# Transposes two steps behind their product, second products three, stores four, in a fused conditional-linear and ternary-FFN kernel

## The chip, the cores and the metric

One NeuronCore of a Trainium2 chip runs the whole program. The metric is the device time of one execution in microseconds, as the median of several runs. The engines are TensorE (PE in the profile; its weight loads are PEld), VectorE (DVE), ScalarE (ACT), GpSimd (POOL) and SyncE (SP), which here only issues DMAs.

## What is computed

128 elements of 128 rows and 512 columns. Each element has a category (0 to 63), which picks a 512x512 matrix and a bias. The result goes through a linear layer whose weights are rounded to -1, 0, 1 and whose activations are rounded to 8 bits by row; the output is added to x. Cut to what matters:

```python
cond = einsum('bsd,bdh->bsh', x, W[itok]) + b[itok][:, None, :]
w_scale = mean(abs(weight)) + 1e-8
w_quant = clip(round(weight / w_scale), -1, 1)
a_scale = max(abs(cond), axis=-1, keepdims=True) + 1e-8
a_quant = round(clip(cond / a_scale * 127, -128, 127))
y = einsum('bsi,oi->bso', a_quant, w_quant) * (w_scale * a_scale / 127)
out = x + y
```

## The kernel before

The kernel sorts the elements by category first, so that the weights of a category are loaded once, and writes the order into a table in SBUF (element numbers, "new category" flags, offsets into the rings of weights and biases). Then come 128 steps, one element each. `over_steps` writes them out as 8 first steps, a loop of 14 groups of 8, and 8 last steps; r is the step, u its place in the group.

A float32 product is done as three products of split operands (hi x hi, hi x lo, lo x hi). What each engine does in its step r, in the order in which it is written:

- **TensorE** (`body`, line 601): reads the offset of its weights from the table into a register (line 603, through `row_of`, line 165), waits for x_lo, for the seeded bias and for w_lo of step r, and issues the 12 matmuls of the **product** (lines 619 to 621) into one of four PSUM banks, `cond_ps`. Then `a_transpose(r-1)` (4 transposes, line 597, waits for the rounding of r-1 and for a free aT bank) and `second_product(r-2)` (4 matmuls, line 587, waits for `aT_moved` of r-2 and for the result of r-4, which frees one of two y banks).
- **VectorE** (`body`, line 523): absmax over the finished product r (line 527), step size and its inverse (lines 530, 533), `result(r-2)` (line 520: y times its scale plus x, in place in `x_rows`), then, only if step r+3 brings a new category, `split_low(r+3)`: two pieces of w_lo = w_raw - w_hi (line 486).
- **ScalarE** (`body`, line 399): `move(r-1)` (line 396, transposed values from PSUM to SBUF as bf16, waits for the transposes), the **rounding** of r (line 406, waits for the inverse), the **seed** of r+2 (line 346: the bias is copied into the bank of the product two steps ahead, `SEED_AHEAD` = 2), then, if step r+4 brings a new category, `split_high(r+4)`: two pieces of w_hi (line 355).
- **GpSimd** (`body`, line 323): splits x of step r+2 into x_hi and x_lo (lines 315, 317), and makes the output scale of r from absmax (line 334).
- **SyncE** (`body`, line 272), one queue: the store of r-3 (line 210, `STORE_BEHIND` = 3, waits for the result), then loads: transposed x of r+5 (waits for x_lo of r+1), rows of x of r+1 into a ring of 8 slots (line 284 waits until the store of the slot's last user, step r-7, has landed), and weights and bias of r+6 if they are new (waits for w_lo of r+2).

The rings: 4 slots of weights, 8 of biases, 4 of x, of rounded activations and of aT, 4 of the row scales, 8 of `x_rows`, 4 product banks, 2 banks each for y and aT. All engines run their own queue in order; they are tied by semaphores only. After step 127 the last transposes, second products, results and stores are written out (lines 627 to 630, 408, 545, 290).

Of the kernel before, what the change touches and what calls it, by code (L numbers as in the profile page):

```python
# [26 lines left out]
def adaln_ffn(nc, x, x_t, itok, cond_w, cond_b, ffn_t, out):  # L27
    B, S, D = x.shape
# [6 lines left out]
    U = 8  # L35
    W_RING, BIAS_RING, XT_RING, Q_RING, STAT_RING = 4, 8, 4, 4, 4
    COND_BANKS, PS_RING = 4, 2
    LO_AHEAD, HI_AHEAD, W_AHEAD, XT_AHEAD, ROWS_AHEAD = 3, 4, 6, 5, 1
    X_AHEAD, SEED_AHEAD, Y_BEHIND, STORE_BEHIND = 2, 2, 2, 3
    PIECES = 2  # L40
    PIECE = W_FREE // PIECES
    BUSY = 12
# [2 lines left out]
    with ctx:  # L45
# [293 lines left out]
        @block.scalar  # L339
        def _(act):  # L340
            def bias_slot(step):
                (bias_offset,) = row_of(act, step, BIAS_OFFSET, 1)
                return bounded(act, bias_offset, (BIAS_RING - 1) * H)

            def seed(bias_offset, n):
                act.activation(cond_ps[n % COND_BANKS][:, :], bias[:, bass.ds(bias_offset, H)],  # L346
                               ACT.Copy).then_inc(bias_seeded, 1)

            def split_high(new, offset, step, n):

                with act.If(new > 0):
                    act.wait_ge(w_loaded[n], w_landed(step, n))
                    for piece in range(PIECES):
                        at = offset + piece * PIECE
                        act.activation(w_hi[:, bass.ds(at, PIECE)], w_raw[:, bass.ds(at, PIECE)],  # L355
                                       ACT.Copy).then_inc(w_hi_done, 1)
                with act.Else():

                    if type(step) is not int or step > 1:
                        act.wait_ge(w_hi_done, (step - 1) * PIECES)  # L360
                    act.sem_inc(w_hi_done, PIECES)

            act.wait_ge(consts_done, 3)
            act.activation(marks[:, 0:1], rounder[:, :], ACT.Abs)
            act.wait_ge(elements_mm_done, 1)
            for column, behind in ((XT_ELEMENT, W_AHEAD - XT_AHEAD), (ROWS_ELEMENT, W_AHEAD - ROWS_AHEAD),
                                   (OUT_ELEMENT, W_AHEAD + STORE_BEHIND)):
                act.activation(table[:, behind:behind + B, column], y_ps[1][0:1, 0:B],
                               ACT.Copy).then_inc(elements_done, 1)
            act.wait_ge(ffn_loaded, 16)  # L370
            act.activation(ffn_abs[:, :], ffn_raw[:, :], ACT.Abs,
                           accum_out=ffn_sum[:, 0:1]).then_inc(ffn_summed, 1)
            for k in range(KD):
                act.wait_ge(w0_loaded[k], 16)
                act.activation(w_hi[:, k * H:(k + 1) * H], w_raw[:, k * H:(k + 1) * H],
                               ACT.Copy).then_inc(w0_hi_done, 1)
                if k == 0:
                    act.wait_ge(banks_opened, COND_BANKS)
                    act.wait_ge(bias0_loaded, 16)
                    seed(0, 0)  # L380
            act.wait_ge(table_done, 1)
            for step in range(1, HI_AHEAD):
                new, offset = w_slot(act, step)
                if step < SEED_AHEAD:
                    bias_offset = bias_slot(step)
                split_high(new, offset, step, step)
                if step < SEED_AHEAD:
                    act.wait_ge(w_loaded[step], 32)
                    seed(bias_offset, step)

            def move(step, n, first):

                act.wait_ge(aT_done, step + 1)
                if not first or n >= Q_RING:
                    act.wait_ge(y_mm_done, step - Q_RING + 1)
                act.activation(aT[:, n % Q_RING, :], aT_ps[n % PS_RING][:, 0:H].bitcast(I16), ACT.Copy,  # L396
                               bias=-HALF_OFFSET).then_inc(aT_moved, 1)

            def body(r0, u, first, last):
                r = r0 + u  # L400
                if not first or u:
                    move(r - 1, (u - 1) % U, first)
                if not first or u >= Q_RING:
                    act.wait_ge(aT_done, r - Q_RING + 1)
                act.wait_ge(a_inv_done, r + 1)
                act.activation(a_rounded[:, u % Q_RING, :], cond_ps[u % COND_BANKS][:, :], ACT.Identity,  # L406
                               bias=rounder[:, 0:1], scale=a_inv[:, u % STAT_RING:u % STAT_RING + 1]).then_inc(a_rounded_done, 1)
                if last and u == U - 1:
                    move(r, u, False)
                if not last or u + SEED_AHEAD < U:  # L410
                    bias_offset = bias_slot(r + SEED_AHEAD)
                    n = (u + SEED_AHEAD) % U
                    act.wait_ge(w_loaded[n], w_landed(r + SEED_AHEAD, n))
                    seed(bias_offset, n)
                if not last or u + HI_AHEAD < U:
                    new, offset = w_slot(act, r + HI_AHEAD)
                    split_high(new, offset, r + HI_AHEAD, (u + HI_AHEAD) % U)

            over_steps(act, body)

        @block.vector
        def _(dve):
# [100 lines left out]
            def body(r0, u, first, last):  # L523
                r = r0 + u
                s = u % STAT_RING
                dve.wait_ge(cond_mm_done, r + 1)
                dve.tensor_reduce(absmax[:, s:s + 1], cond_ps[u % COND_BANKS][:, :], AX.X, ALU.max,  # L527
                                  apply_absolute_value=True).then_inc(absmax_done, 1)
                dve.wait_ge(absmax_done, r + 1)
                dve.tensor_scalar(a_step[:, s:s + 1], absmax[:, s:s + 1], EPS, 1.0 / LEVELS,  # L530
                                  ALU.add, ALU.mult).then_inc(a_step_done, 1)
                dve.wait_ge(a_step_done, r + 1)
                dve.reciprocal(a_inv[:, s:s + 1], a_step[:, s:s + 1]).then_inc(a_inv_done, 1)  # L533
                if first and u == 0:
                    ternary_begin()
                elif first and u == 1:
                    ternary_end()
                else:
                    result(r - Y_BEHIND, (u - Y_BEHIND) % U)
                if not last or u + LO_AHEAD < U:  # L540
                    new, offset = w_slot(dve, r + LO_AHEAD)
                    split_low(new, offset, r + LO_AHEAD)
# [6 lines left out]
        def _(pe):  # L549
# [51 lines left out]
            def body(r0, u, first, last):  # L601
                r = r0 + u
                _, offset = w_slot(pe, r)
                start = first and u == 0
                pe.wait_ge(x_lo_done, r + 1)
                pe.wait_ge(bias_seeded, r + 1)
                n = u % XT_RING
                for k in range(KD):
                    if start:
                        pe.wait_ge(w0_lo_done, k + 1)  # L610
                    elif k * PIECES % KD == 0:

                        pe.wait_ge(w_lo_done, (r - 1) * PIECES + k * PIECES // KD + 1)
                    x_hi_k = xT_hi[:, n, k * P:(k + 1) * P]
                    x_lo_k = xT_lo[:, n, k * P:(k + 1) * P]
                    w_hi_k = w_hi[:, bass.ds(offset + k * H, H)]
                    w_lo_k = w_lo[:, bass.ds(offset + k * H, H)]
                    ps_cond = cond_ps[u % COND_BANKS][:, :]
                    pe.matmul(ps_cond, x_hi_k, w_hi_k, start=False, stop=False, skip_group_check=True)  # L619
                    pe.matmul(ps_cond, x_hi_k, w_lo_k, start=False, stop=False, skip_group_check=True)  # L620
                    last_mm = pe.matmul(ps_cond, x_lo_k, w_hi_k, start=False, stop=(k == KD - 1), skip_group_check=True)  # L621
                last_mm.then_inc(cond_mm_done, 1)
                if not first or u >= 1:
                    a_transpose(r - 1, (u - 1) % U, first)
                if not first or u >= Y_BEHIND:
                    second_product(r - Y_BEHIND, (u - Y_BEHIND) % U, first)
                if last and u == U - 1:
                    second_product(r - 1, u - 1, False)
                    a_transpose(r, u, False)
                    second_product(r, u, False)  # L630

            over_steps(pe, body)


# [24 lines left out]
```

## Time and profile before

| | |
|---|---|
| median of 3 runs (lowest, highest) | 546.17 us (544.36, 547.55) |
| profiled execution | 543.38 us, span 541.5 us |
| TensorE busy | 512.7 us (95%) |
| VectorE busy | 392.5 us (72%) |
| ScalarE busy | 343.7 us (63%) |
| GpSimd busy | 281.2 us (52%) |
| moved by DMA | 172.76 MB, mean 319 GB/s |
| mean granted TensorE clock | 0.998 of full speed |

The span is the time from the first to the last instruction on the core. Matmuls overlap in the pipeline, and their ends are modelled, so 95% busy does not mean that TensorE issues without gaps: the starts of successive matmuls tell more. A wait in the list of waits is the idle time of an engine just ahead of an instruction, with the last releaser that the trace knows; "issue" means that it knows none. Names with q (PEldq, DVEq) are an engine's sequencer, which reads registers and waits, and is not counted as busy.

### The profile page before, as it was taken

The page shows a single profiled execution, that of the slowest core. Times are in us where ns is not written, and L with a number is a line of the kernel's source. Part 1 is how long each engine was busy: PE and PEld are TensorE (multiplying, and loading weights), DVE is VectorE, ACT ScalarE, POOL GpSimd, SP SyncE. Part 2 cuts the span into 40 slices and gives each one's busy share as a digit, 9 for nine tenths or more (in the row PEclk, how much of TensorE's full clock was granted, in tenths as well). Part 3 has the DMA queues.
Part 4 walks back from the last instruction along what each step waited for, and adds up shares of the span by engine and source line. Part 5 has one row for each costly group of instructions (what it writes and reads, how often), then busy time and mean ns, then how long its engine had stood idle before and what let it go on. Part 6 is the DMA issues. An engine that isn't in the chain of part 4 may idle for free.

```text
span 541.5 us, 13855 instructions
## 1 busy us (share of the span) xinstructions
PE 512.7 (95%) x2584; PEld 355.8 (66%) x2585; DVE 392.5 (72%) x652; ACT 343.7 (63%) x502; POOL 281.2 (52%) x396
## 2 busy tenths in 40 slices
PE   4799999999999999999999998999989999999996
PEld 1576667666776666677676665667657677777774
DVE  3787765879667968966866858776797868758763
ACT  3577565765676567666756666766766666666753
POOL 3695455444556364555554463555446455565540
PEclk9999999999999999999999999999999999999999
DMA  5899879998899999979989889987999999899963
GB/s 170 276 404 351 291 258 310 382 364 274 324 364 343 367 333 392 356 243 372 350 291 294 325 322 398 365 288 271 407 332 363 329 363 342 273 310 333 323 194 117
DMA packets 71728, 172.76 MB, mean 319 GB/s; under 512 B 8096, under 2 KB 8224, under 8 KB 64800
## 3 DMA queue, kind: packets, MB, share of 16 engines
q1 hardware_dynamic: 71712, 172.59, 90.0%
q8 instruction: 5, 0.08, 0.1%
q14 instruction: 11, 0.09, 0.1%
HBM read 139.00 MB, written 33.55 MB: 319 GB/s over the span
## 4 chain that ended last, share of the span: by engine, by line
PE 35%; DVE 6%; issue 5%; DVEq 2%; ACT 2%; DMA 2%; ACTq 0%; SPq 0%; POOL 0%; POOLq 0%
PE ps_cond L619 9%; PE ps_cond L621 8%; PE ps_cond L620 8%; PE ps_y L587 8%; DVE sb_w_lo L486 3%; PE ps_aT L597 2%; DVE sb_absmax L527 2%; DMA sb_bias<-cond_b 2%; DVEq L165 1%; ACT sb_a_rounded L406 1%; ACT sb_w_hi L355 1%; DVE sb_a_step L530 0%; ACTq L165 0%; DVE sb_x_rows L520 0%; DVEq L486 0%
## 5 line engine op out<-in xcount | busy, mean ns | idle before, releaser
L619 PE MATMUL ps_cond<-sb_w_hi,sb_xT_hi 128*128 x512 | 220.7, 431 | 6.7 <-issue 3.2
L621 PE MATMUL ps_cond<-sb_w_hi,sb_xT_lo 128*128 x512 | 200.3, 391 | 0.0
L620 PE MATMUL ps_cond<-sb_w_lo,sb_xT_hi 128*128 x512 | 199.4, 389 | 0.0
L486 DVE TENSOR_TENSOR sb_w_lo<-sb_w_raw,sb_w_hi x106 | 162.1, 1567 | 20.2 <-issue 16.8
L317 POOL TENSOR_TENSOR sb_xT_lo<-sb_xT_raw,sb_xT_hi 128x512 fp32r<-128x512 f32 x128 | 166.4, 1300 | 10.9
L527 DVE TENSOR_REDUCE sb_absmax<-ps_cond 128x1 f32<-128x512 f32 x128 | 87.7, 686 | 100.6 <-PE ps_cond L621 89.1
L406 ACT ACTIVATE sb_a_rounded<-ps_cond,sb_rounder,sb_a_inv 128x512 f32<-128x512 f32 x128 | 99.5, 777 | 94.9 <-DVE sb_a_inv L533 94.5
L334 POOL TENSOR_SCALAR sb_y_scale<-sb_absmax,sb_w_step 128x1 f32<-128x1 f32 x128 | 41.0, 320 | 224.6 <-DVE sb_absmax L527 224.3
L587 PE MATMUL ps_y<-sb_ffnT,sb_aT 128*128 128x512 bf16 x512 | 131.2, 379 | 1.6 <-DVE sb_ffnT L512 0.9
L619 PEld LDWEIGHTS ps_cond<-sb_w_hi,sb_xT_hi 128*128 128x128 f32 x512 | 96.2, 188 | 51.7 <-issue 27.2
L396 ACT ACTIVATE sb_aT<-ps_aT 128x512 bf16<-128x512 int16 x128 | 75.4, 589 | 67.5 <-PE ps_aT L597 62.8
L355 ACT ACTIVATE sb_w_hi<-sb_w_raw x106 | 106.3, 1051 | 14.9 <-issue 9.2
L621 PEld LDWEIGHTS ps_cond<-sb_w_hi,sb_xT_lo 128*128 128x128 f32 x512 | 96.0, 188 | 21.7
L620 PEld LDWEIGHTS ps_cond<-sb_w_lo,sb_xT_hi 128*128 128x128 f32 x512 | 96.4, 188 | 18.0
L520 DVE SCALAR_TENSOR_TENSOR sb_x_rows<-ps_y,sb_y_scale,sb_x_rows 128x512 f32<-128x512 f32 x128 | 96.1, 751 | 6.4 <-PE ps_y L587 1.7
L315 POOL CAST sb_xT_hi<-sb_xT_raw 128x512 fp32r<-128x512 f32 x128 | 78.2, 611 | 17.8 <-DMA sb_xT_raw<-x_t 12.5
L346 ACT ACTIVATE ps_cond<-sb_bias 128x512 f32 (+1 forms) x128 | 76.2, 595 | 7.6 <-issue 6.2
L587 PEld LDWEIGHTS ps_y<-sb_ffnT,sb_aT 128*128 128x128 bf16 x512 | 44.6, 98 | 32.4 <-ACT sb_aT L396 1.2
L597 PE MATMUL ps_aT<-sb_ident_bf,sb_a_rounded 128*128 128x128 bf16 x512 | 50.9, 222 | 9.9 <-ACT sb_a_rounded L406 9.7
L597 PEld LDWEIGHTS ps_aT<-sb_ident_bf,sb_a_rounded 128*128 128x128 bf16 x512 | 29.0, 98 | 46.3 <-issue 24.8
L533 DVE RECIPROCAL sb_a_inv<-sb_a_step 128x1 f32<-128x1 f32 x128 | 20.9, 164 | 4.4
L530 DVE TENSOR_SCALAR sb_a_step<-sb_absmax 128x1 f32<-128x1 f32 x128 | 19.7, 154 | 4.4
(69 smaller groups left out, 36.2 us busy)
## 6 DMA issues: line engine op xcount, KB each, us to landing
sb_w_raw<-cond_w SPq DMA_DIRECT2D x53, 1024.0 KB, 6.6
sb_xT_raw<-x_t SPq DMA_DIRECT2D x128, 256.0 KB, 5.1
sb_x_rows<-x SPq DMA_DIRECT2D x128, 256.0 KB, 5.2
out<-sb_x_rows SPq DMA_DIRECT2D x128, 256.0 KB, 4.9
sb_bias<-cond_b SPq DMA_DIRECT2D x54, 256.0 KB, 7.9
sb_ffn_raw<-ffn_t SPq DMA_DIRECT2D x1, 1024.0 KB, 6.9
sb_w_raw<-cond_w SPq DMA_DIRECT2D x4, 256.0 KB, 6.7
sb_cat_row_i<-itok SPq DMA_DIRECT2D x1, 64.0 KB, 3.5
```

The source lines that it names most:

```text
L315: pool.tensor_copy(xT_hi[:, m, :], xT_raw[:, m, :]).then_inc(x_hi_done, 1)
L317: pool.tensor_tensor(xT_lo[:, m, :], xT_raw[:, m, :], xT_hi[:, m, :].bitcast(F32), ALU.subtract).then_inc(x_lo_done, 1)
L355: act.activation(w_hi[:, bass.ds(at, PIECE)], w_raw[:, bass.ds(at, PIECE)], ACT.Copy).then_inc(w_hi_done, 1)
L406: act.activation(a_rounded[:, u % Q_RING, :], cond_ps[u % COND_BANKS][:, :], ACT.Identity, bias=rounder[:, 0:1], scale=a_inv[:, u % STAT_R ...
L486: dve.tensor_tensor(w_lo[:, bass.ds(at, PIECE)], w_raw[:, bass.ds(at, PIECE)], w_hi[:, bass.ds(at, PIECE)].bitcast(F32), ALU.subtract).the ...
L520: dve.scalar_tensor_tensor(x_rows[:, n, :], y_ps[n % PS_RING][:, :], y_scale[:, s:s + 1], x_rows[:, n, :], ALU.mult, ALU.add).then_inc(y_d ...
L527: dve.tensor_reduce(absmax[:, s:s + 1], cond_ps[u % COND_BANKS][:, :], AX.X, ALU.max, apply_absolute_value=True).then_inc(absmax_done, 1)
L587: last_mm = pe.matmul(y_ps[n % PS_RING][:, :], aT[:, n % Q_RING, k * P:(k + 1) * P], ffnT[:, k, :], start=(k == 0), stop=(k == KH - 1))
L597: last_t = pe.transpose(aT_ps[n % PS_RING][:, k * P:(k + 1) * P], low[:, k * P:(k + 1) * P, 0], ident_bf[:, :])
L619: pe.matmul(ps_cond, x_hi_k, w_hi_k, start=False, stop=False, skip_group_check=True)
L620: pe.matmul(ps_cond, x_hi_k, w_lo_k, start=False, stop=False, skip_group_check=True)
L621: last_mm = pe.matmul(ps_cond, x_lo_k, w_hi_k, start=False, stop=(k == KD - 1), skip_group_check=True)
```

## The change

`T_BEHIND` = 2 is new: in step r TensorE transposes the rounded activation of r-2 instead of r-1, and ScalarE moves that of r-2. `Y_BEHIND` goes from 2 to 3: TensorE does the second product, and VectorE the result, of r-3 instead of r-2. `STORE_BEHIND` goes from 3 to 4, which also makes the table one row longer. The first steps leave out what isn't there yet, and after the last step one more transposition, second product, move and result are written out. Ring sizes and how far ahead anything is loaded, split or seeded stay.

```diff
--- before.py
+++ after.py
@@ -36,7 +36,7 @@
     W_RING, BIAS_RING, XT_RING, Q_RING, STAT_RING = 4, 8, 4, 4, 4
     COND_BANKS, PS_RING = 4, 2
     LO_AHEAD, HI_AHEAD, W_AHEAD, XT_AHEAD, ROWS_AHEAD = 3, 4, 6, 5, 1
-    X_AHEAD, SEED_AHEAD, Y_BEHIND, STORE_BEHIND = 2, 2, 2, 3
+    X_AHEAD, SEED_AHEAD, T_BEHIND, Y_BEHIND, STORE_BEHIND = 2, 2, 2, 3, 4
     PIECES = 2
     PIECE = W_FREE // PIECES
     BUSY = 12
@@ -398,15 +398,16 @@
 
             def body(r0, u, first, last):
                 r = r0 + u
-                if not first or u:
-                    move(r - 1, (u - 1) % U, first)
+                if not first or u >= T_BEHIND:
+                    move(r - T_BEHIND, (u - T_BEHIND) % U, first)
                 if not first or u >= Q_RING:
                     act.wait_ge(aT_done, r - Q_RING + 1)
                 act.wait_ge(a_inv_done, r + 1)
                 act.activation(a_rounded[:, u % Q_RING, :], cond_ps[u % COND_BANKS][:, :], ACT.Identity,
                                bias=rounder[:, 0:1], scale=a_inv[:, u % STAT_RING:u % STAT_RING + 1]).then_inc(a_rounded_done, 1)
                 if last and u == U - 1:
-                    move(r, u, False)
+                    for n in range(U - T_BEHIND, U):
+                        move(B - U + n, n, False)
                 if not last or u + SEED_AHEAD < U:
                     bias_offset = bias_slot(r + SEED_AHEAD)
                     n = (u + SEED_AHEAD) % U
@@ -535,7 +536,7 @@
                     ternary_begin()
                 elif first and u == 1:
                     ternary_end()
-                else:
+                elif not first or u >= Y_BEHIND:
                     result(r - Y_BEHIND, (u - Y_BEHIND) % U)
                 if not last or u + LO_AHEAD < U:
                     new, offset = w_slot(dve, r + LO_AHEAD)
@@ -620,11 +621,13 @@
                     pe.matmul(ps_cond, x_hi_k, w_lo_k, start=False, stop=False, skip_group_check=True)
                     last_mm = pe.matmul(ps_cond, x_lo_k, w_hi_k, start=False, stop=(k == KD - 1), skip_group_check=True)
                 last_mm.then_inc(cond_mm_done, 1)
-                if not first or u >= 1:
-                    a_transpose(r - 1, (u - 1) % U, first)
+                if not first or u >= T_BEHIND:
+                    a_transpose(r - T_BEHIND, (u - T_BEHIND) % U, first)
                 if not first or u >= Y_BEHIND:
                     second_product(r - Y_BEHIND, (u - Y_BEHIND) % U, first)
                 if last and u == U - 1:
+                    a_transpose(r - 1, u - 1, False)
+                    second_product(r - 2, u - 2, False)
                     second_product(r - 1, u - 1, False)
                     a_transpose(r, u, False)
                     second_product(r, u, False)
```

## Rows read from the trace of the kernel before

**Rows 1.** The page: span, busy time of each engine (share) xinstructions, DMA totals.
```profile
span 541.5 us, 13855 instructions
...
PE 512.7 (95%) x2584; PEld 355.8 (66%) x2585; DVE 392.5 (72%) x652; ACT 343.7 (63%) x502; POOL 281.2 (52%) x396
...
DMA packets 71728, 172.76 MB, mean 319 GB/s; under 512 B 8096, under 2 KB 8224, under 8 KB 64800
```

**Rows 2.** The page, chain that ended last: shares of the span by engine.
```profile
PE 35%; DVE 6%; issue 5%; DVEq 2%; ACT 2%; DMA 2%; ACTq 0%; SPq 0%; POOL 0%; POOLq 0%
```

**Rows 3.** Waits, whole span: engine and line waited for, total us, times, longest.
```profile
PEld ps_cond L619 <- issue: 27.2, 52, 1.5
...
PE ps_aT L597 <- ACT sb_a_rounded L406: 9.7, 14, 1.0
```

**Rows 4.** Timeline of PE: first matmuls of products 6, 126 and 127 (start us, us).
```profile
39.32 0.58 PE L619 MATMUL ps_cond<-sb_w_hi,sb_xT_hi 128*128 x1
...
527.00 0.58 PE L619 MATMUL ps_cond<-sb_w_hi,sb_xT_hi 128*128 x1
...
530.85 0.58 PE L619 MATMUL ps_cond<-sb_w_hi,sb_xT_hi 128*128 x1
```

**Rows 5.** Timeline of PE: product 27, transposes, second product, product 28.
```profile
124.67 0.53 PE L619 MATMUL ps_cond<-sb_w_hi,sb_xT_hi 128*128 x1
...
128.65 0.40 PE L597 MATMUL ps_aT<-sb_ident_bf,sb_a_rounded 128*128 128x128 bf16 x4 [0.94 <-ACT sb_a_rounded L406]
128.89 1.03 PE L587 MATMUL ps_y<-sb_ffnT,sb_aT 128*128 128x512 bf16 x4
129.90 0.49 PE L619 MATMUL ps_cond<-sb_w_hi,sb_xT_hi 128*128 x1
```

**Rows 6.** Timeline of VectorE over three of its steps.
```profile
121.45 0.68 DVE L527 TENSOR_REDUCE sb_absmax<-ps_cond 128x1 f32<-128x512 f32 x1
...
123.44 3.29 DVE L486 TENSOR_TENSOR sb_w_lo<-sb_w_raw,sb_w_hi  x2 [0.23 <-issue]
126.66 0.68 DVE L527 TENSOR_REDUCE sb_absmax<-ps_cond 128x1 f32<-128x512 f32 x1
...
128.85 0.69 DVE L527 TENSOR_REDUCE sb_absmax<-ps_cond 128x1 f32<-128x512 f32 x1 [0.36 <-DVEq L492]
```

**Rows 7.** The page, groups of instructions: VectorE splits of weights.
```profile
L486 DVE TENSOR_TENSOR sb_w_lo<-sb_w_raw,sb_w_hi x106 | 162.1, 1567 | 20.2 <-issue 16.8
```

**Rows 8.** Timeline of ScalarE: rounding and bias seed.
```profile
127.82 0.78 ACT L406 ACTIVATE sb_a_rounded<-ps_cond,sb_rounder,sb_a_inv 128x512 f32<-128x512 f32 x1 [3.01 <-DVE sb_a_inv L533]
128.50 0.59 ACT L346 ACTIVATE ps_cond<-sb_bias 128x512 f32 x1
```

**Rows 9.** Source line 165, PE's sequencer (ns min/median/max): whole span, then 49.9 to 50.1.
```profile
L165 PEldq TENSOR_LOAD <-sb_table x128: 532/538/2149, 11.5 to 528.4; - x128
...
L165 PEldq TENSOR_LOAD <-sb_table x1: 1467/1467/1467, 50.0 to 50.0; - x1
```

**Rows 10.** Timeline of PE in the first steps, before product 3.
```profile
25.73 0.40 PE L597 MATMUL ps_aT<-sb_ident_bf,sb_a_rounded 128*128 128x128 bf16 x4
27.05 1.02 PE L587 MATMUL ps_y<-sb_ffnT,sb_aT 128*128 128x512 bf16 x4 [0.92 <-DVE sb_ffnT L512]
27.86 0.50 PE L619 MATMUL ps_cond<-sb_w_hi,sb_xT_hi 128*128 x1
```

**Rows 11.** Windows: first steps (last columns: PEclk, DMA share, GB/s).
```profile
22.90:39.30 16.40, 15.48 (x83) 10.97 (x81) 14.34 (x21) 11.50 (x17) 15.97 (x14) 1.00 1.00 373
```

**Rows 12.** Timeline of the end: ScalarE, PE, VectorE.
```profile
535.16 0.78 ACT L406 ACTIVATE sb_a_rounded<-ps_cond,sb_rounder,sb_a_inv 128x512 f32<-128x512 f32 x1 [0.34 <-DVE sb_a_inv L533]
...
537.08 1.04 PE L587 MATMUL ps_y<-sb_ffnT,sb_aT 128*128 128x512 bf16 x4 [0.69 <-ACT sb_aT L396]
...
538.15 0.75 DVE L520 SCALAR_TENSOR_TENSOR sb_x_rows<-ps_y,sb_y_scale,sb_x_rows 128x512 f32<-128x512 f32 x1 [1.45 <-PE ps_y L587]
```

**Rows 13.** Source line 210, stores: us from issue to landing.
```profile
DMA to landing us min/median/max: 2.0/4.9/8.1
```

## The prediction

> **What bounds the kernel now.** The page comes first: TensorE is busy for 95% of 541.5 us, VectorE for 72%, and 172.76 MB move at a mean of 319 GB/s [rows 1]. A mean like that hides stages, so the chain of waits comes next. PE holds 35% of it, and the rest of what can be named is mostly VectorE and "issue" [rows 2]. In the list of waits the reader is to see two kinds of PE stall: transposes that wait for the rounding (9.7 us, 14 times, none over 1.0), and the first weight load of a product, which waits for nothing that the profile shows (27.2 us, 52 times) [rows 3]. Second, the pace. An undisturbed step is 3.85 us, from product to product [rows 4]. Product 6 starts at 39.32 and product 127 at 530.85 [rows 4]: 491.5 us for 121 steps, which undisturbed would be 465.3. So the middle of the kernel holds **26.3 us of stall**. That is what can be won there.
>
> Where does it come from? A VectorE step that also splits weights lasts 5.21 us (absmax at 121.45, the next one at 126.66); one that does not can be followed by the next absmax after 2.19 (126.66 to 128.85) [rows 6]. 106 pieces of w_lo are 53 splitting steps [rows 7]. In the timeline they fall into 22 single ones, 11 pairs and 3 triples. One split puts VectorE 5.21 - 3.85 = 1.36 us behind PE, and the next plain step makes it good. Two in a row put it 2.7 behind, and then PE stops. Product 27 starts at 124.67, and its 12 matmuls are over in time for transposes 2.9 us later, but these start at 128.65, released by the rounding. Then come second product and the next product, at 129.90: 5.23 us for the step, **1.38 lost** [rows 5]. 11 pairs at 1.38, and 3 triples at 1.38 + 1.36 = 2.74, are 23.4 of the 26.3 us. 2.9 are left for single splits and for register loads.
>
> **The change, part by part.**
>
> *Transposes two steps behind.* No instruction is added. Each step still has its 12 matmuls, 4 transposes and 4 matmuls of the second product, so the floor of 3.85 stays, and PE cannot gain from it. What goes is the wait: after product r the transposes want the rounding of r-2, a whole step old, not that of r-1. What is late next? The bias that ScalarE copies into the bank of product r+1. It stands behind the same rounding in ScalarE's queue, since it is seeded two steps ahead, as before. In the stalled step the rounding starts at 127.82, the seed at 128.50, and the seed ends at 129.09 [rows 8]. Without the change the following product starts at 129.90 [rows 5]. With it, the transposes and the second product run while the seed is awaited, and the product starts as soon as the seed is there. How long after it the trace doesn't show. The lower bound is the 0.05 from the end of a rounding (127.82 + 0.78) to the transposes at 128.65; the upper bound is a whole register load of 0.54 [rows 9]. I take 0.35, nearer the upper end because PE's sequencer still has the product's other waits and address computations to do. So 129.44 for 129.90: **0.46 us** (0.27 to 0.76).
>
> This is won once for each backlog, not once a step. While VectorE is behind without a break, its own 5.21 a step sets the pace, and a PE that can run further ahead only moves the start of the stall. So 11 + 3 = 14 times 0.46 = **6.4 us** (3.8 to 10.6).
>
> *The sequencer's lead.* Ahead of each product PE's sequencer reads the table of offsets: 538 ns in the median, but up to 2149, and one of 1467 stands for several others [rows 9]. Its long cases are hidden only if it is reached early, and the sequencer reaches it after the waits of the transposes. Today these end with the rounding of r-1, so after any single split (VectorE 1.36 late) the read comes late and its excess shows as "issue" [rows 3]. Afterwards the wait ahead of it is for a move of aT which ScalarE does ahead of that rounding. With the 0.05 to 0.15 that a single split costs, this is what the remaining 2.9 us are made of. I take **2.0** (0 to 2.9).
> The Trainium skill (TensorE: Matmul & The Clock Gate, Architectural detail) gives TensorE a queue of 64 instructions, which is more than the 40 loads and matmuls of a step. By that rule the sequencer could be a step ahead, all long reads would vanish, and this term would be 2.9. No row here shows the depth of the queue.
>
> *Second products three steps behind, in VectorE too.* VectorE's result(r-3) stands where result(r-2) stood, and its second product is again the one that PE issues in the same step, so this wait keeps its place. The second product waits for the move of r-3, which ScalarE does at the head of step r-1, as it did that of r-2 before. The bank of y is freed by the result of r-5 in VectorE's step r-2, as before. The four-slot rings of aT, a_rounded and of the scales are enough, and no bank of cond is held longer. Cost 0. All of it lies beside PE's products.
>
> *Start.* Step 1 has no transposes, step 2 no second product. Today the second product of row 0 stands there until ternary ffnT is done (27.05, idle 0.92), and product 3 starts at 27.86, although the transposes ahead were issued at 25.73 [rows 10]. Afterwards product 3 can start at 25.73 + 0.23 = 25.96. It keeps up to 1.9, for VectorE loses its result in step 2 as well (0.75) and so isn't the next bound. But the DMA engines are busy for a share of 1.00 in this stretch [rows 11], and the loads may hold it: I take **1.5** (0 to 1.9).
>
> *End.* One more transposition and second product are left over. The move of 126 now stands behind the rounding of 127 in ScalarE's queue (535.16 + 0.78). So it runs from about 535.8 to 536.4, second product 126 from 536.5 to 537.3, transposes 127 after that, their move to 538.4, and the last second product starts at about 538.45 instead of 537.08 [rows 12]. **1.4 us lost** (1.1 to 1.6), and the last result at 538.15 moves with it.
>
> *Stores four behind.* SP waits for y_done of r-4, which VectorE sets in step r-1, as it did for r-3: the wait is not later. The loads of x_t, x and weights behind it in SP's queue keep their places. What gets shorter is the time from a store to the reuse of its x_rows slot: three steps, 11.5 us, instead of four. The slowest store landed after 8.1 us [rows 13]. Cost 0; if that cover were gone, SP would stand there with the weight load behind it.
>
> **Sum**: 6.4 + 2.0 + 1.5 - 1.4 = **8.5 us**. The profiled execution was 543.4 us (span 541.5 and 1.9 around it) and would be 534.9. The median of the runs is 546.17, 2.8 above it. I set the gain against it: **537.7**. By the ends of the terms: 3.8 + 0 + 0 - 1.6 = 2.2 to 10.6 + 2.9 + 1.9 - 1.1 = 14.3, that is 531.9 to 544.0.
>
> **The rivals.**
> *The seed takes the whole place of the rounding.* If a product that was held by its seed starts as late as it does now (0.8 us after the seed's end), the 14 backlogs give nothing. For: both hang on one rounding, 0.68 us apart. Against: 1.25 us of PE work lies between transposes and product, and now overlaps the wait. Start and end cancel: about 546.
>
> *The transfers are the bound where weights come thick.* For: the share of 1.00 at the start [rows 11], a mean of 319 GB/s [rows 1]. Pairs and triples are just where a megabyte of weights a step is loaded. Against: among the longest waits of VectorE and ScalarE none of size is for a DMA. Half of the backlogs' gain and the start would go: 537.7 + 3.2 + 1.5 = 542.4.
> The Trainium skill (Perfetto Trace Analysis, Roofline) puts the ceiling of one core's 16 DMA engines at about 435 GB/s. By it 172.76 MB need some 397 us, and this rival has room only in short stretches.
>
> *Slower: the stores.* With a slot needed again after 11.5 us, a store that lands later stops SP, and with it the weight loads behind. It decides from a landing of 11.2 us on, 3.1 above the slowest. Prefetch of six steps absorbs the first of it. If each of the 14 dense stretches then loses 1 us: 546.2 - 8.5 + 14 = 551.7.
>
> *More than forecast*: seeds hardly hold PE and all long reads are hidden: 532 to 533.
>
> **How the numbers follow.** Forecast 0.72, seeds 0.10, transfers 0.09, stores 0.05, more 0.04. A difference of under 0.5% (2.7 us) can't be told from none here. Faster by more than that, under 543.4: nearly all of the forecast, about all of "more" and half of "transfers", 0.81. Within it 0.14, slower 0.05. The range of 8 in 10 is 533.5 to 544.0.
>
> **What would show it right or wrong.** Transposes have no wait for the rounding left in the list of waits. Steps that come after pairs of splits take 4.7 to 4.8 us instead of 5.2, and the wait moves to L619. PE's 121 steps from product 6 to 127 take 483 us instead of 491.5. The last second product starts some 7.6 us after the last product, instead of 6.2 (537.08 less 530.85). It is wrong if steps after pairs stay at 5.2, if ScalarE's w_hi starts to wait for DMA, or if SP waits for stores within the loop.

## The result, and the profile after

The changed kernel takes **538.49 us** (median of 4 runs, 537.63 to 540.65) against 545.81 for the kernel before (4 runs, 544.36 to 547.55). The ratio is 0.987, with a 95% interval from 0.984 to 0.990: 7.3 us faster, forecast 8.5. The predicted 537.7 is 0.8 us off. The profiled execution went from 543.38 to 539.01, its span from 541.5 to 537.2. That is 4.4 us and not 7.3, because the profiled execution of before was quicker than all four of its timed runs (544.36 and up). So what is read below from one pair of traces is checked, where it matters, against the other traces of kernels with the same lag.

First the page and the waits of the changed kernel, which answer to [rows 1] and [rows 3]. Line numbers behind the change are one higher than before: 598 are the transposes, 588 the second product, 620 to 622 the product.

```profile
span 537.2 us, 13884 instructions
...
PE 508.2 (95%) x2584; PEld 356.9 (66%) x2585; DVE 386.9 (72%) x652; ACT 343.2 (64%) x502; POOL 280.2 (52%) x396
```

```profile
PEld ps_cond L620 <- issue: 31.4, 33, 2.0
...
PE ps_cond L620 <- ACT ps_cond L346: 10.7, 14, 1.6
ACT sb_w_hi L355 <- DMA sb_bias<-cond_b: 7.8, 8, 1.4
...
PEld ps_aT L598 <- ACT sb_a_rounded L406: 7.1, 27, 0.3
```

The transposes' wait for the rounding has left PE's own list. What remains of it on PEld is never over 0.3 us. In its place a new row stands: 14 times the product waits for its seed, 10.7 us in all. (The row with "issue" doesn't mean that no cause is known: its longest cases are weight loads of products whose first matmul shows the seed.) ScalarE's waits of w_hi for a transfer are 7.8 us, 8 times; before they were 4.0 us, 5 times. The prediction had named this as a sign of being wrong; it is there, but small.

The stalled step of [rows 5] and [rows 8] in the changed kernel, first PE, then ScalarE:

```profile
122.79 0.58 PE L620 MATMUL ps_cond<-sb_w_hi,sb_xT_hi 128*128 x1
...
125.72 0.40 PE L598 MATMUL ps_aT<-sb_ident_bf,sb_a_rounded 128*128 128x128 bf16 x4
125.96 1.03 PE L588 MATMUL ps_y<-sb_ffnT,sb_aT 128*128 128x512 bf16 x4
127.60 0.49 PE L620 MATMUL ps_cond<-sb_w_hi,sb_xT_hi 128*128 x1 [0.62 <-ACT ps_cond L346]
```

```profile
125.99 0.78 ACT L406 ACTIVATE sb_a_rounded<-ps_cond,sb_rounder,sb_a_inv 128x512 f32<-128x512 f32 x1 [2.13 <-DVE sb_a_inv L534]
126.67 0.59 ACT L346 ACTIVATE ps_cond<-sb_bias 128x512 f32 x1
```

The transposes run 2.93 us after the product's start, although the rounding for which they waited before, that of product 26, only begins at 125.99. The seed ends at 127.26, and the product follows 0.34 us later. The step lasts 4.81 us instead of 5.23.

Products 6 and 127, which answer to [rows 4]:

```profile
39.31 0.58 PE L620 MATMUL ps_cond<-sb_w_hi,sb_xT_hi 128*128 x1
...
525.13 0.58 PE L620 MATMUL ps_cond<-sb_w_hi,sb_xT_hi 128*128 x1
```

The 121 steps between take 485.8 us instead of 491.5, that is **20.6 us over the floor** instead of 26.3. Forecast was 483. (The floor of 465.3 is 121 steps of 3.845 us; the median step of either trace is 3.847.) Single traces differ by about 1 us here, so three of each kind are worth a look. With transposes one step behind, the loss over the floor is 26.3 us in the kernel before and 27.6 in each of two variants below that time the same (a part of the change, and the seed first). With two behind it is 20.6 in the changed kernel and 19.5 and 20.4 in two variants that time the same (the early read, and second products four behind). The means are 27.2 and 20.2: **7.0 us**, which fits the medians better than 5.7.

### The profile page after: what moved, and what is told of

Read it like the earlier page. It is cut to its first block and busy times, and to the rows that moved or that the text cites. A ratio compares the mean times of both kernels' runs of the same rounds, so it can differ in the third digit from the quotient of the medians.

```text
span 537.2 us, 13884 instructions
## 1 busy us (share of the span) xinstructions
PE 508.2 (95%) x2584; PEld 356.9 (66%) x2585; DVE 386.9 (72%) x652; ACT 343.2 (64%) x502; POOL 280.2 (52%) x396
## 5 line engine op out<-in xcount | busy, mean ns | idle before, releaser
L620 PE MATMUL ps_cond<-sb_w_hi,sb_xT_hi 128*128 x512 | 221.9, 433 | 16.7 <-ACT ps_cond L346 10.7
L487 DVE TENSOR_TENSOR sb_w_lo<-sb_w_raw,sb_w_hi x106 | 156.2, 1512 | 28.8 <-issue 22.0
L355 ACT ACTIVATE sb_w_hi<-sb_w_raw x106 | 106.4, 1052 | 20.6 <-issue 11.2
```

The lines of the kernel that those rows point to most:

```text
L487: dve.tensor_tensor(w_lo[:, bass.ds(at, PIECE)], w_raw[:, bass.ds(at, PIECE)], w_hi[:, bass.ds(at, PIECE)].bitcast(F32), ALU.subtract).the ...
```

## The experiments

Each was timed in turn with the kernel before on the same chip, and its ratio is to the kernel before of that session, whose median was 547.21, 545.88, 546.01 and 545.26 us in the four sessions. Differences to the changed kernel are between sessions: they are good to 1 or 2 us.

**Only a part: transposes stay one step behind.**

```diff
-    X_AHEAD, SEED_AHEAD, T_BEHIND, Y_BEHIND, STORE_BEHIND = 2, 2, 2, 3, 4
+    X_AHEAD, SEED_AHEAD, T_BEHIND, Y_BEHIND, STORE_BEHIND = 2, 2, 1, 3, 4
...
-                    a_transpose(r - 1, u - 1, False)
```

> Only a part of the change: second products three steps behind and stores four, but transposes one step behind, as before. Theory (the gain comes from the transposes' wait alone): 545 to 548, no gain in the middle, the transposes still wait for the rounding some 14 times. Rival (the second product's wait for the move, or the result's place on VectorE, was part of what held PE): at least half of the 7 us gained.

547.64 us, ratio 1.002 (0.999 to 1.005). As expected, nothing is gained, and the wait is what it was before:

```profile
PEld ps_aT L598 <- ACT sb_a_rounded L406: 25.5, 41, 2.2
...
PE ps_aT L598 <- ACT sb_a_rounded L406: 12.5, 14, 1.8
```

**Only a part: stores four behind on the kernel before.**

```diff
-    X_AHEAD, SEED_AHEAD, Y_BEHIND, STORE_BEHIND = 2, 2, 2, 3
+    X_AHEAD, SEED_AHEAD, Y_BEHIND, STORE_BEHIND = 2, 2, 2, 4
```

> The kernel before with the stores alone four steps behind; second products two, transposes one. SP then waits for a result made a step earlier. With stores three behind on the changed kernel ScalarE waited 91 us for weights, so SP's place against VectorE matters. Theory (loads are held by w_lo, their ring's release, in the same VectorE step, as soon as the store does not hold them): within 1.5 us of before. Rival (SP's waits of 26.1 us for results delay the weights already in the kernel before, and part of the change's gain is the store's alone): 3 us or more faster than before.

547.86 us, ratio 1.005 (1.003 to 1.007): no gain, but a loss of 2 us, a little more than the theory's 1.5. Its cause was not looked for. The stores alone are no part of the gain.

**The change without its part on the stores.**

```diff
-    X_AHEAD, SEED_AHEAD, T_BEHIND, Y_BEHIND, STORE_BEHIND = 2, 2, 2, 3, 4
+    X_AHEAD, SEED_AHEAD, T_BEHIND, Y_BEHIND, STORE_BEHIND = 2, 2, 2, 3, 3
```

> The changed kernel with stores three steps behind instead of four: SP then waits for a result that VectorE makes in the same step and not in the one before, with the loads behind it in SP's queue. Theory (loads have steps of slack): within 1.5 us of the changed kernel, 537 to 541. Rival (SP's queue is late enough that weights arrive late; four behind is a needed part of the change): 3 us or more slower than the changed kernel.

563.67 us, ratio 1.029 (1.024 to 1.035). The theory fell by far: this is some 25 us slower than the changed kernel. Waits of SP, then of ScalarE:

```profile
SPq L210 <- DVE sb_x_rows L521: 66.2, 47, 3.5
```

```profile
ACT sb_w_hi L355 <- DMA sb_bias<-cond_b: 91.1, 51, 5.1
```

SP now waits for a result of the same VectorE step (66.2 us; in the changed kernel 21.7), and the weight load stands behind this wait in its queue. ScalarE then waits 91.1 us for weights instead of 7.8. The six steps of prefetch are no slack here: a load can only be issued when the split of w_lo has freed its slot, and with one more VectorE step of delay behind that the weights come too late.

**One step more for the stores.** The same line with `STORE_BEHIND` = 5.

> The changed kernel with stores five steps behind. SP no longer waits for a result (21.7 us, 19 times in the changed kernel), but a slot of x_rows is needed again two steps, 7.7 us, after its store was issued, and the slowest of before landed after 8.1. Theory (loads are held by the release of the weight ring, and nearly all stores land in time): within 2 us of the changed kernel. Rival one (the store's slot decides): 4 us or more slower, with waits of SP for stores. Rival two (SP's waits for results cost time): 3 us or more faster.

541.24 us, ratio 0.989 (0.985 to 0.994), so the changed kernel's time within the noise, or up to 3 us more. SP's wait for results fell to 13.0 us, and its wait for the split rose from 14.6 to 25.1, so the loads leave no earlier. SP never waited for a store's slot inside the loop:

```profile
SPq L230 <- DVE sb_w_lo L487: 25.1, 15, 2.9
SPq L210 <- DVE sb_x_rows L521: 13.0, 9, 3.0
```

**The seed ahead of the rounding, in the changed kernel.**

```diff
             def body(r0, u, first, last):
                 r = r0 + u
+                if not last or u + SEED_AHEAD < U:
+                    bias_offset = bias_slot(r + SEED_AHEAD)
+                    n = (u + SEED_AHEAD) % U
+                    if not first or u + SEED_AHEAD >= COND_BANKS:
+                        act.wait_ge(a_rounded_done, r + SEED_AHEAD - COND_BANKS + 1)
+                    act.wait_ge(w_loaded[n], w_landed(r + SEED_AHEAD, n))
+                    seed(bias_offset, n)
                 if not first or u >= T_BEHIND:
                     move(r - T_BEHIND, (u - T_BEHIND) % U, first)
...
-                if not last or u + SEED_AHEAD < U:
-                    bias_offset = bias_slot(r + SEED_AHEAD)
-                    n = (u + SEED_AHEAD) % U
-                    act.wait_ge(w_loaded[n], w_landed(r + SEED_AHEAD, n))
-                    seed(bias_offset, n)
```

> The changed kernel, but ScalarE seeds the bank of step r+2 at the head of its step r, ahead of the move and of the rounding of r. Theory (the seed behind the rounding holds PE where VectorE is late: 14 waits of the product for the seed, 10.7 us, and 0.34 us from the seed's end to the product in each): the product's wait for the seed goes, steps after a pair of splits fall from 4.8 us to near 3.85, and the whole falls by 8 to 15 us against the changed kernel, to 524 to 531. Rival (VectorE's 5.21 us per splitting step is the bound wherever splits are dense, so no queue order can help): within 2 us of the changed kernel.

532.23 us, ratio 0.973 (0.968 to 0.977): 6.3 us under the changed kernel by the medians, 7.9 by the ratios. The direction is the theory's, the size just short of it. Between products 6 and 127 the loss over the floor is 14.1 us. PE's wait for the seed is down from 10.7 to 1.3 us, and two others have come forward:

```profile
ACT sb_w_hi L355 <- DMA sb_bias<-cond_b: 26.2, 27, 2.0
...
PEld ps_y L590 <- ACT sb_aT L396: 8.3, 11, 1.6
...
PE ps_y L590 <- ACT sb_aT L396: 6.0, 10, 1.4
...
PE ps_cond L622 <- ACT ps_cond L346: 1.3, 2, 0.8
```

**The same in the kernel before.**

> The kernel before, with the same move of the seed to the head of ScalarE's step. Theory (transposes one step behind wait for the rounding of VectorE's late step, whatever the seed does): no gain, 544 to 548, and steps after a pair stay at 5.2 us. Rival (it was the seed all along that held PE, and the lag of the transposes is only a small part): some 8 us or more faster than before.

547.02 us, ratio 0.998 (0.996 to 1.001). No gain, as expected. The transposes' lag and the seed's place hold the same backlog one behind the other. Taking away the second alone gives nothing, and taking away the first alone only uncovers the second.

**A further step for the second products, with the seed first.**

```diff
-    W_RING, BIAS_RING, XT_RING, Q_RING, STAT_RING = 4, 8, 4, 4, 4
+    W_RING, BIAS_RING, XT_RING, Q_RING, STAT_RING = 4, 8, 4, 4, 8
...
-    LO_AHEAD, HI_AHEAD, W_AHEAD, XT_AHEAD, ROWS_AHEAD = 3, 4, 6, 5, 1
-    X_AHEAD, SEED_AHEAD, T_BEHIND, Y_BEHIND, STORE_BEHIND = 2, 2, 2, 3, 4
+    LO_AHEAD, HI_AHEAD, W_AHEAD, XT_AHEAD, ROWS_AHEAD = 3, 4, 6, 5, 0
+    X_AHEAD, SEED_AHEAD, T_BEHIND, Y_BEHIND, STORE_BEHIND = 2, 2, 2, 4, 5
...
-            load_rows(element, 0)
...
+                    second_product(r - 3, u - 3, False)
```

> The changed kernel with the seed first, second products and results four steps behind, stores five; rows of x are loaded in their own step instead of one ahead, which keeps three steps between a store and the reuse of its slot, and the row scales have 8 slots. With the seed first, the second product waits 14.3 us for the move of aT (8.3 of its weight loads, 6.0 of its matmuls), which stands behind w_hi. Theory (that move is the next bound): 3 to 7 us faster than with the seed first alone (532.2), 525 to 529. Rival (ScalarE is held by weights from DMA, 26.2 us, and the stall moves to the next instruction): within 1.5 us of 532.

526.55 us, ratio 0.963 (0.959 to 0.967). The theory holds: 5.7 us under the seed alone by the medians, 5.1 by the ratios. The waits for the move fell from 8.3 and 6.0 us to:

```profile
PEld ps_y L589 <- ACT sb_aT L395: 0.9, 1, 0.9
...
PE ps_y L589 <- ACT sb_aT L395: 0.7, 1, 0.7
```

**The further step without the seed.** The same, but the seed back behind the rounding.

> As the run with second products four behind (526.6), but the seed back behind the rounding: the changed kernel with second products and results four steps behind, stores five, rows of x loaded in their own step, 8 slots of row scales. Theory (in the changed kernel the seed is the bound, the move of aT only behind it): within 2 us of the changed kernel, 537 to 540, with the product's waits for the seed as before. Rival (the further lag is what gives, the seed's place matters little): 530 or less.

538.37 us, ratio 0.986 (0.982 to 0.989): the changed kernel's time. The further lag, with the rows of x and the slots that go with it, gives nothing while the seed is the bound:

```profile
PE ps_cond L619 <- ACT ps_cond L345: 12.9, 16, 1.3
```

**The early read, in the kernel before.**

```diff
+            ahead = [None]
...
-                _, offset = w_slot(pe, r)
+                _, offset = w_slot(pe, r) if u == 0 else ahead[0]
...
                 last_mm.then_inc(cond_mm_done, 1)
+                if u + 1 < U:
+                    ahead[0] = w_slot(pe, r + 1)
```

> The kernel before, but TensorE's sequencer reads the next product's offset from the table right after the product, ahead of the waits of transposes and second product (in seven of eight steps). Theory (a late read, long by chance, cost the kernel before some 2 us, up to 5 with what a read of 0.54 adds behind each held transpose): 2 to 5 us faster than before, 541 to 545. Rival (these reads are hidden or fall where VectorE decides anyway): within 1 us of before.

542.92 us, ratio 0.992 (0.990 to 0.995): 3.0 us faster by the medians, 4.2 by the ratio. The profiled executions show less: product 6 at 39.83 and product 127 at 530.77, so 490.9 us against 491.5 before. What the read costs is plain in the stalled step of [rows 5]. First this kernel (its product 27 starts at 125.42), then the read ahead of product 28 in the kernel before:

```profile
129.45 0.40 PE L597 MATMUL ps_aT<-sb_ident_bf,sb_a_rounded 128*128 128x128 bf16 x4 [0.93 <-ACT sb_a_rounded L406]
129.68 1.03 PE L587 MATMUL ps_y<-sb_ffnT,sb_aT 128*128 128x512 bf16 x4
130.36 0.58 PE L621 MATMUL ps_cond<-sb_w_hi,sb_xT_hi 128*128 x1
```

```profile
L165 PEldq TENSOR_LOAD <-sb_table x1: 537/537/537, 128.9 to 128.9; - x1
```

From the held transposes to the product 0.91 us pass here, as in an undisturbed step (3.85 less 2.94). In the kernel before 1.25 pass (128.65 to 129.90), because the read starts only with the transposes, takes 0.54, and the product starts 0.45 after its end. So even a read of ordinary length costs 0.34 us behind each held transpose. It is no single case: 47 steps of the kernel before between products 6 and 127 last over 3.88 us, and in all of them the next product starts 0.45 to 0.57 us after the end of its read.

**The early read, in the changed kernel.**

> The changed kernel with TensorE's offset read right after the product. On the kernel before this gave 0.8% (4.2 us). Theory (part of the change's 7.3 us is this same lead of the sequencer, and the two overlap): at most 1.5 us faster than the changed kernel (some 538.5). Rival (the early read is a gain of its own, independent of the change): again some 4 us, 534 to 535.

538.51 us, ratio 0.986 (0.983 to 0.989), against 538.49 without it: nothing. The change already holds this gain.

**Seed first, second products four behind, and the early read.**

> Seed first, second products four behind, and the early read of the offset. Theory (with no early wait ahead of it the read is hidden unless the product's own waits come late): 0 to 2 us faster than 526.6. Rival (the waits of transposes and moves still hold the sequencer): 3 us or more faster.

524.64 us, ratio 0.961 (0.958 to 0.965). This is the fastest of all, 3.9% under the kernel before and 13.9 us under the changed one. The step from 526.55 is within what these runs can tell.

**Half of VectorE's split left out, in the changed kernel.** Half of the columns of w_lo are not computed and stay zero.

```diff
+            begin(dve.memset(w_lo[:, :].bitcast(F32), 0.0))
             dve.wait_ge(cat_row_loaded, 16)
...
-                        dve.tensor_tensor(w_lo[:, bass.ds(at, PIECE)], w_raw[:, bass.ds(at, PIECE)],
-                                          w_hi[:, bass.ds(at, PIECE)].bitcast(F32), ALU.subtract).then_inc(w_lo_done, 1)
+                        dve.tensor_tensor(w_lo[:, bass.ds(at, PIECE // 2)], w_raw[:, bass.ds(at, PIECE // 2)],
+                                          w_hi[:, bass.ds(at, PIECE // 2)].bitcast(F32), ALU.subtract).then_inc(w_lo_done, 1)
```

> The changed kernel with half of VectorE's split left out: each piece of w_lo computes half of its columns, the others stay zero (w_lo is zeroed once at the start, which lengthens the start by some us). This leaves a part of the float32 product out. Theory (what PE still loses after the change, 20.6 us between product 6 and 127, comes from VectorE's 5.2 us per splitting step): the stretch from product 6 to 127 falls from 485.8 us to 466 to 470, near the floor of 465.3. Rival (the weights' transfers or ScalarE's w_hi are the bound in the dense stretches): it stays above 478.

529.58 us, ratio 0.972 (0.968 to 0.975). The whole time holds a longer start, since w_lo is zeroed first (product 6 at 43.66 instead of 39.31), so the stretch behind it is what counts. Products 6 and 127 of this run:

```profile
43.66 0.58 PE L621 MATMUL ps_cond<-sb_w_hi,sb_xT_hi 128*128 x1
...
515.01 0.58 PE L621 MATMUL ps_cond<-sb_w_hi,sb_xT_hi 128*128 x1
```

471.4 us between them instead of 485.8, that is 6.1 over the floor. A little above the 466 to 470 of the theory and far below the rival's 478. So 14.5 of the 20.6 us that PE still loses go when VectorE's split is halved. A splitting step of VectorE, from absmax to absmax, mostly takes 4.16 us here, still more than 3.85, so the half that is left can be part of the rest. ScalarE's waits for weights rose to 26.4 us, so transfers are a candidate too; that was not separated. Nor is the loss fixed by VectorE: with the whole split, the seed first and second products four behind, products 6 and 127 are 473.9 us apart, 8.6 over the floor.

## Why the prediction was right, and which terms were not

**Transposes two behind: what is waited for is right, the price of one clean stall too, but partly for another reason, and the sum of 14 is not.** A product starts 0.34 us after its seed (taken: 0.35), and the clean case gains 0.42 us (taken: 0.46): from product 27 at 122.79 to 28 at 127.60. But the 1.25 us between held transposes and product, which the prediction calls PE's work, are not that: the work is 0.91, and 0.34 is the register read behind the transposes, as the early read shows. Without it the product of [rows 5] would have started at 129.56, only 0.12 after the forecast 129.44. So some three quarters of the 0.46 are the sequencer's lead, the second term of the sum, and not the transposes' wait as such. That 0.46 fits is in part luck.

And 14 x 0.46 = 6.4 did not come. Only four of the stalls behind pairs and triples last 4.8 to 4.9 us, as forecast (products 27, 37, 72 and 100). Six last 5.1 to 5.9, so the sign "4.7 to 4.8 instead of 5.2" holds for the clean cases alone. I took the product starts of both traces and summed all steps in which two splitting steps of VectorE stand in a row, and the two steps behind (42 steps): they lose 20.7 us over the floor before and 21.1 after. The other 79 steps lose 5.6 us over the floor before; after, they stand 0.5 us under it. So in this pair of traces the dense stretches gained **nothing in sum**, and the rest gained 6.1. Over three traces of each kind, those of the section on the result, the dense stretches gained 1.3 us (21.9 to 20.6) and the rest 5.7 (5.3 to -0.4). What PE gains ahead of a backlog it hands back there, since its product then waits for a seed that hangs on VectorE. Products 8, 9 and 10, before, then after, show it:

```profile
47.01 0.58 PE L619 MATMUL ps_cond<-sb_w_hi,sb_xT_hi 128*128 x1
...
51.91 0.49 PE L619 MATMUL ps_cond<-sb_w_hi,sb_xT_hi 128*128 x1 [0.70 <-POOL sb_xT_lo L317]
...
55.67 0.58 PE L619 MATMUL ps_cond<-sb_w_hi,sb_xT_hi 128*128 x1
```

```profile
47.01 0.58 PE L620 MATMUL ps_cond<-sb_w_hi,sb_xT_hi 128*128 x1
...
50.85 0.58 PE L620 MATMUL ps_cond<-sb_w_hi,sb_xT_hi 128*128 x1
...
55.51 0.49 PE L620 MATMUL ps_cond<-sb_w_hi,sb_xT_hi 128*128 x1 [0.46 <-ACT ps_cond L346]
```

1.06 us are gained with product 9, and 0.90 of them are gone with product 10, which waits for its seed. (The row of before names GpSimd's x_lo as what ended the wait of product 9. But x_lo of product 9 was ready at 45.55; the one that ends just then is that of product 10. The read ended at 51.46, 0.45 ahead of the product.)

The prediction gave the reason as VectorE's 5.21 us a step, against which a PE that runs further ahead only moves its stall. That is half of it. With the seed first, the same 42 steps lose 6.4 us instead of 21.1, with VectorE's splits as they were: a backlog of two or three splits is short, and PE can run past it if nothing that it needs hangs on VectorE's current step. In the changed kernel the seed still did.

**The sequencer's lead: right in kind, sized at a third.** I took 2.0 us with a ceiling of 2.9, because I had booked 23.4 of the 26.3 us to pairs and triples. Outside them 6.1 us were won, 5.7 over three traces each. The read ahead of product 9 is the example: in [rows 9] it took 1.467 us and started 3.0 us after product 8. Now it starts 0.8 us after it:

```profile
L165 PEldq TENSOR_LOAD <-sb_table x1: 542/542/542, 47.8 to 47.8; - x1
```

Part of this is luck, since here the read was also short. Nor are all long reads hidden now: in the changed kernel product 78 comes 5.88 us after product 77, since its read took 2.03 us and started 3.4 us after product 77. But the early read alone makes the kernel before 0.8% faster and the changed one not at all, which shows that the lead is worth having and that the change brings it. Both mis-sized terms lie in the middle and nearly cancel: 8.4 forecast for it, 5.7 in these two traces and 7.0 over three each. In this pair of traces the steps outside the backlogs gave 6.1 us, and the backlogs took 0.3. Of the 6.1, 5.2 stand before at seven products whose reads took over 0.7 us.

**Second products and results three behind, at no cost: right.** Without the transposes' lag they change nothing (547.64).

**Start: 1.5 forecast, 0 in this pair of traces, 1.1 over all.** Product 3 came at 26.28 instead of 27.86, near the 25.96 of the prediction. But product 5 stands at 35.54 against 35.47, and product 6 at 39.31 against 39.32: the lead was gone again. ScalarE's splits wait for their transfers in this stretch in both traces (1.04 and 1.11 us before, 0.81 and 1.29 after), which fits the prediction's remark that the loads may hold it; it was not tested. And the start varies between executions. In the five traces with transposes one behind, product 6 stands at 39.32 to 41.12, mean 40.2; in the five with transposes two behind, second products three behind and nothing new at the start, at 38.93 to 39.31, mean 39.2. So about 1.1 us is won, and the profiled execution of before had a quick start. Start and middle together, 1.1 + 7.0, less 1.4 at the end, are 6.7 us, near the 7.3 of the medians.

**End: right to 0.06.** The last second product and result, which answer to [rows 12]:

```profile
532.70 1.04 PE L588 MATMUL ps_y<-sb_ffnT,sb_aT 128*128 128x512 bf16 x4 [0.69 <-ACT sb_aT L396]
```

```profile
533.78 0.75 DVE L521 SCALAR_TENSOR_TENSOR sb_x_rows<-ps_y,sb_y_scale,sb_x_rows 128x512 f32<-128x512 f32 x1 [1.20 <-PE ps_y L588]
```

532.70 - 525.13 = 7.57 us from the last product to the last second product, instead of 6.23: 1.34 lost, forecast 1.4.

**Stores: no cost can be seen in the change, but the cover was misnamed.** On the kernel before the further step of the stores alone cost 2 us, so 0 isn't shown by itself. The wait kept its place only because it went one step back together with the result. I had said that six steps of prefetch would absorb a late SP; the run with stores three behind lost 25 us to just that. The shorter time to the reuse of a slot, which I had made the slower rival, does not matter here: with two steps instead of three the kernel took 541.24 us and SP waited for no slot.

Of the rivals, the seed was the nearest to what happened. It is the new bound, though not at the whole price of the old. Its 546 left out the sequencer's 2.0 without a reason, and its "against", the 1.25 us of PE work, was the misreading above. Waits for transfers grow once PE is quicker: 26.2 us of ScalarE's waits with the seed first, against 7.8 in the changed kernel. What they cost PE was not measured.

## What to carry to other kernels

When a consumer waits for a late producer, look what else stands behind the same producer in its queue. Here the lag of the transposes paid 7 us, much of it by letting a register read run early, and a second instruction behind the same rounding held back another 6 to 8. The two only pay in this order: the seed first without the lag gave nothing. Don't multiply the gain of one stall by their number where another engine's work fills the stretch. Before such a sum, ask whether that engine ever idles between the stalls, and what else still ties yours to its current step. And a step taken out of phase with a queue that also issues loads can cost more than the whole change brings.

## What the runs showed of the hardware

The read of a register from SBUF by TensorE's sequencer takes 532 ns at best and 538 (before) or 539 (changed) in the median, but up to 2149 ns before and 2307 in the changed kernel; 23 and 35 of the 128 take over 700 ns. It is no instruction of the busy share, and it shows as "issue". In both kernels a product that had waited for the read started 0.45 to 0.57 us after the end of it. Where the read stands in the sequencer's order decides whether it costs anything; placed right behind the product it made the kernel before 0.8% faster (0.5 to 1.0).

From the end of a seed on ScalarE to the first matmul of the product that waited for it, 0.34 us pass in the clean cases; from the end of a rounding to the transposes that waited for it, 0.05 [rows 5, 8]. The product has its sequencer's own waits and address computations behind the semaphore, the transposes have none; that this makes the difference is my reading, and no run shows it.
